# Norm squares stored in another token order, and an own timetable for the last group of a half

## The reference

```python
y = jnp.moveaxis(ys, 0, 1) + x * D[None, None, :, None]
yg = y.reshape(B, L, G, GROUP_SIZE)
var = jnp.mean(yg * yg, axis=-1, keepdims=True)
yn = (yg * lax.rsqrt(var + EPS)).reshape(B, L, I) * norm_weight
yn = yn * jax.nn.silu(gate)
out = jnp.einsum('bli,di->bld', yn, out_proj_w)
```

## Time and profile before

| | |
|---|---|
| time of 3 runs, median (lowest to highest) | 3199.41 us (3190.49 to 3212.25) |
| the profiled execution's own time | 3210.87 us |
| its span, first to last instruction | 3209.4 us |
| its mean granted TensorE clock | 0.975 |
| busy share PE / DVE / ACT / POOL | 95% / 67% / 52% / 20% |
| first half, second half, output block | about 0 to 1240, 1240 to 2473, 2473 to 3209 us |

### The profile page before, as it was taken

One profiled execution on the slowest core, in us unless ns is written; L12 is line 12 of the kernel. 1 busy time (PEld: TensorE's weight loads), 2 busy tenths in 40 slices (PEclk: granted clock), 3 DMA queues, 4 the chain that ended last, 5 costly groups with the idle time before them and its releaser, 6 DMA issues. The chain is left out here.

```text
span 3209.4 us, 44961 instructions
## 1 busy us (share of the span) xinstructions
PE 3064.5 (95%) x14304; PEld 2387.6 (74%) x14304; DVE 2155.3 (67%) x2660; ACT 1684.9 (52%) x3716; POOL 633.8 (20%) x447
## 2 busy tenths in 40 slices
PE   7999999999999994999999999999995999999998
PEld 6777777777777764777777777777773788888776
DVE  7666667675756664767666666767573887668877
ACT  3566574755656571475655756575563323234433
POOL 3222212121212223412112221212123000001112
PEclk9999999999999996999999999999997999999999
DMA  3434343343434333433352434334342444456565
GB/s 129 142 135 154 102 151 102 137 144 111 148 107 145 119 114 114 144 133 126 111 171 99 154 104 148 105 138 147 105 153 91 137 143 141 147 177 226 203 212 173
DMA packets 125815, 444.90 MB, mean 139 GB/s; under 512 B 17776, under 2 KB 22000, under 8 KB 109296
## 3 DMA queue, kind: packets, MB, share of 16 engines
q1 hardware_dynamic: 117840, 423.18, 39.4%
q0 software_dynamic: 4096, 14.68, 1.2%
q10 hardware_dynamic: 3744, 5.51, 0.5%
HBM read 397.90 MB, written 45.42 MB: 138 GB/s over the span
## 5 line engine op out<-in xcount | busy, mean ns | idle before, releaser
L935 PE MATMUL bank<-x_hi,w_hi 128*128 128x512 f32 x2560 | 1030.2, 402 | 7.3 <-DVE acc L692 7.3
L937 PE MATMUL bank<-x_hi,w_lo 128*128 128x512 f32 x2560 | 1005.5, 393 | 0.0
L936 PE MATMUL bank<-x_lo,w_hi 128*128 128x512 f32 x2560 | 1002.7, 392 | 0.0
L692 DVE SCALAR_TENSOR_TENSOR acc<-bank,conv_w,acc 128x511 f32<-128x511 f32 (+2 forms) x576 | 431.0, 748 | 352.9 <-ACT acc L521 325.5
L935 PEld LDWEIGHTS bank<-x_hi,w_hi 128*128 128x128 f32 x2560 | 484.3, 189 | 126.4 <-issue 21.8
L937 PEld LDWEIGHTS bank<-x_hi,w_lo 128*128 128x128 f32 x2560 | 484.3, 189 | 105.6
L936 PEld LDWEIGHTS bank<-x_lo,w_hi 128*128 128x128 f32 x2560 | 485.4, 190 | 95.3
L521 ACT ACTIVATE acc<-bank,tap_par 128x512 f32<-128x512 f32 x192 | 149.2, 777 | 654.7 <-PE bank L937 500.6
L1441 PE MATMUL bank<-wo_hi,y_hi 128*128 128x512 f32 x1024 | 401.4, 392 | 40.2 <-DVE wo_lo L1308 36.9
L1442 PE MATMUL bank<-wo_lo,y_hi 128*128 128x512 f32 x1024 | 400.0, 391 | 0.0
L1443 PE MATMUL bank<-wo_hi,y_lo 128*128 128x512 f32 x1024 | 399.8, 390 | 0.0
(11 more groups left out here) (153 smaller groups left out, 3394.8 us busy)
## 6 DMA issues: line engine op xcount, KB each, us to landing
attn<-cum_scratch SPq DMA_DIRECT2D x128, 1280.0 KB, 6.7
w_raw<-in_w_in SPq DMA_DIRECT2D x160, 512.0 KB, 3.6
y_raw<-y_scratch SPq DMA_DIRECT2D x128, 512.0 KB, 3.7
y_scratch<-gate SPq DMA_DIRECT2D x32, 1024.0 KB, 6.4
wo_raw<-in_w_out SPq DMA_DIRECT2D x128, 256.0 KB, 3.8
xbc<-in_x SPq DMA_DIRECT2D x16, 512.0 KB, 4.3
attn<-in_x SPq DMA_DIRECT2D x16, 512.0 KB, 3.7
rstd_b<-rc_scratch SPq DMA_DIRECT2D x32, 256.0 KB, 3.9
```

Of the source, the lines that this page charges most:

```text
L692: dve.scalar_tensor_tensor(acc[:, s % 2, back:], bank_proj[s % 2][:, 0:SEQ - back], mix.conv_w[:, g, m, 3 - back:4 - back], acc[:, s % 2, ...
L935: pe.matmul(out, w_hi[m % 2][:, k, :], hi, start=(k == 0), stop=False)
L936: pe.matmul(out, w_hi[m % 2][:, k, :], lo, start=False, stop=False)
L937: mm = pe.matmul(out, w_lo[m % 2][:, k, :], hi, start=False, stop=(k == KT - 1))
```

## The change

There are two parts. First, ScalarE writes each tile of squares in another order: token `4i + k` goes to column `128k + i`. It still reads `y` in token order, so 4 neighbouring results go 512 bytes apart each. GpSimd's sums are made column by column and are the same work. The weights of channel sum k are then the 128 neighbouring columns from `128k`.

Second, group 7 of each half gets its own plan `LAST`, with other slots for products, loads and exponentials. Products 3 to 7 stand one or two slots earlier (14, 16, 18, 20, 21 for 15, 17, 19, 21, 23), with what is derived from them. The exponentials have a list of their own, in which slots 11 and 18 hold two each.

```diff
-    def __init__(self, cb, load, mult, gate_from):
+    def __init__(self, cb, load, mult, gate_from, exp=None):
...
-        self.exp = [s - 3 + h for s in mult for h in range(2)]
+        self.exp = exp or [s - 3 + h for s in mult for h in range(2)]
...
-DRAIN = max(LATER.store) + 1
+LAST = Plan(cb=[4, 6], load=[4, 5, 7, 10, 12, 14, 15, 17], mult=[9, 11, 13, 14, 16, 18, 20, 21],
+            gate_from=CONV_SLOTS, exp=[6, 7, 8, 9, 10, 11, 11, 12, 13, 14, 15, 16, 17, 18, 18, 19])
+DRAIN = max(LAST.store) + 1
...
-            step(GROUPS - 1, LATER, LATER, True)
+            step(GROUPS - 1, LAST, LATER, True)
...
-                piece(GROUPS - 1, LATER, s)
+                piece(GROUPS - 1, LAST, s)
...
-                act.activation(out, y[:, u % 2, :], ACT.Square, scale=GC ** -0.5).then_inc(squared, 1)
+                act.activation(out.rearrange("p (k i) -> p i k", k=CHUNKS),
+                               y[:, u % 2, :].rearrange("p (i k) -> p i k", k=CHUNKS),
+                               ACT.Square, scale=GC ** -0.5).then_inc(squared, 1)
...
-                by_phase = sums[:, q, :].rearrange("p (i k) -> p k i", k=CHUNKS)
                 for k in range(CHUNKS):
-                    mm = pe.matmul(bank_y[q][:, k:k + 1], by_phase[:, k, :], one, start=True, stop=True)
+                    mm = pe.matmul(bank_y[q][:, k:k + 1], sums[:, q, k * P:(k + 1) * P], one, start=True, stop=True)
```

## The result

Over four runs of each kernel on one chip the time went from a median of 3196.74 us (3190.49 to 3212.25) to 3163.84 us (3159.40 to 3165.46). The ratio is 0.9891, with a 95% interval from 0.9866 to 0.9916: 1.1% faster. A second set on another chip gave 3162.26 us against 3198.03, ratio 0.9890 (0.9871 to 0.9908). The profiled execution took 3164.7 us, with a span of 3163.2. The forecast was 3163 us, between 3150 and 3182. The total came out right within 1 us, and that is in part luck: the timetable was worth less than its term, the channel sums a little more, and 2.8 us are explained by no term.

A forecast was written before the change was run, and what follows sets the result against it. TensorE, busy 95% of the span, was taken as the bound inside the groups. From the profiled execution, 3210.9 - 22.4 - 14.4 - 10.2 + 0.4 = 3164.3 us, stated as 3163 us, range 3150 to 3182.

The forecast's parts named there:

- The channel sums: On TensorE, neighbouring weight columns shorten loads, saving 0.8 us on each of 28 sums inside groups: 22.4 us (17 to 31).
- The falls: Drops of TensorE's clock to 0.5 behind channel sums following a product: all nine go, 1.6 us each, 14.4 us.
- The last group: At each half's end, unit 7's product starts 5.3 us sooner, less 0.2 for SP's queue: 10.2 us over two halves.
- the cover for its packed slots: Ahead of the drain, two exponential steps fit slots averaging 7.1 us: nothing charged; without that cover 3 us per half.
- `LAST` stalls an engine: Rival: ScalarE's packed slots delay gate work, or swapped DMAs cost most of 3.9 us; 3 us per half lost, 3169; 10%.
- The SP queue: In the drain, sequence 0's read back now stands behind sequence 1's store: 0.2 us a half charged, at worst 3.9.
- The strided write: ScalarE's scattered square write costs 0.2 us more each; two of 128 lie on a path: 0.4 us (0 to 0.8).

The follow-up runs named there:

- the doubled sums: The changed kernel with each channel sum computed twice from the neighbouring weights, same result: 3190.52 us over eight runs, 3191.33 in a one-run repeat.
- the exponentials moved: The changed kernel with one number changed in `LAST`, the first exponential step of unit 3 back from slot 11 to slot 12: 3158.06 us, ratio 0.9880.
- the timetable alone: The changed kernel with squares and weights put back as before, keeping only `LAST`: 3192.4 us against 3198.34 for the kernel before, ratio 0.9980.
- the strided read: The changed kernel with ScalarE's square reading `y` at a 16-byte stride and writing neighbouring columns: 3160.91 us against 3162.26.

## Why the prediction held, point by point

**The channel sums were right, slightly undersized.** Forecast: a pair 0.107 us apart in place of 0.207, 28 x 0.8 = 22.4 us. Measured: 0.101 behind a projection (0.81/8), so 16 x (1.66 - 0.81) + 12 x (1.89 - 0.92) = 25.2 us. The load's length came out as read from its unstrided neighbour, 192 against 190 ns. That this goes one for one into the time is shown by the doubled sums, and neighbouring groups stand 139.9 us apart where 140.1 was forecast. The Trainium skill (Advanced Engine Details and Errata, SBUF Cachelines) speaks of a penalty when each access goes to a different 16-byte line, and this pair of kernels agrees with it on the loads, 330 against 192 ns.

**The falls were right for the profiled execution and wrong for the median.** All nine went, worth 14.4 us there. That falls stay away behind the short sums is shown (none at 72 boundaries, against 21 at 48 with the strided ones); whether for their length or for their stride is open. The prediction guessed that the number of falls makes the runs' spread, and nonetheless took all nine off. Against a median run only some 5 to 6 us could be won. This didn't spoil the time forecast, as the sum was made against the slow execution that had the nine; it would have misled someone who put the same 14.4 us against the median. Between the execution with 9 falls and the first profile after, the output projection starts 2481.28 - 2435.57 = 45.7 us sooner, and the sum of terms was 46.6.

**The last group: the mechanism and its size were right, the cover for its packed slots wasn't.** Per half the forecast was 5.3 us less 0.2; the drain gives 5.2, and the last product takes 4.53 us behind a wait of 4.35, as assumed. The step that failed is "Ahead of the drain `LAST` packs ScalarE ... I charge nothing". It argued by the length of the slot, 7.1 us, and what bound was the order within it: the weight split stands behind the second step of exponentials (3.0 us), with VectorE's weighing behind that, which costs the product 1.2 us of wait; and this step at times waits for a table that hasn't landed, up to 1.5 us more. The rival *`LAST` stalls an engine* thus came true in part, by the double step that it named and a DMA wait that it didn't. It was priced at 3 us a half. Read at the start of the output projection, the timetable brings 2440.30 - 2430.32 = 10.0 us with the exponentials moved, as forecast (10.2), and 4.7 to 7.4 us as the change has it. The stall gives back 2.6 to 5.3 us over both halves, most of it in the first. The whole times agree: the timetable alone took 3187.23 us in its profile without a fall, 5.4 us less than the 3192.6 of the kernel before less its falls.

**The SP queue cost nothing**, where 0.2 us a half was charged. From the product of unit 7 to the read back (L338) it is 1195.92 - 1184.51 = 11.4 us against 1218.33 - 1207.37 = 11.0 before. Between the first store (L333, now L335) and this read back it is 1.41 us in both (1218.33 - 1216.92 and 1195.92 - 1194.51), so the 0.4 us more lies ahead of the queue, about what the longer square takes (0.45).

**The strided write was mis-sized, outside its own bounds.** Forecast 0.2 us a square, 0.4 at most; measured 0.50 (622 to 1121 ns), 0.98 ns per value. The bound came from a VectorE sum at 0.78 ns per value, and this is another engine. It cost little, because the step that decides was right: only two squares lie on a path, 0.9 us in all. Here the Trainium skill's rule on lines agreed in direction on both sides of ScalarE, as the strided read shows (1102 ns) beside the scattered write (1121 ns), and gives no size.

**What cancelled.** Against the sum of 3164.3 us for the profiled execution: the channel sums 2.8 us better, the last group 5.5 us worse (4.7 in place of 10.2), the squares 0.5 worse. That would be 3167.5; the profiled execution took 3164.7, and the 2.8 us between them aren't explained. Of these 0.8 (235.28 - 234.46) were won ahead of the first channel sum, which the change doesn't touch. Less their falls, executions of the kernel before differ by 3.9 us too (3196.5 and 3192.6 above). By the terms as measured the forecast would have been 4.5 us too low, well inside its range; so the match to 1 us is luck and the range is not. For the medians the same accounting is 25.2 for the sums, 5 to 6 for the falls, 4.7 to 7.4 for the last group and 0.9 back for the squares: 34 to 38 us, where 33 and 36 were measured.

## What to carry to other kernels

Read the weight loads apart from the matmuls: with one moving column the load was the cost here, and weights that lie in every fourth column doubled the time of a channel sum (0.207 us a pair against 0.101); move the stride to an engine that has room: ScalarE paid 60.7 us more in all, and 0.9 of it is found on a path. When a timetable is packed, look for what stands behind each moved step on its engine, and then for whether its input has landed, not for how full the slot is: one number in a list gave back 2.6 to 5.3 of the 10.0 us that the timetable was worth. And before something in one profile is counted as a gain, ask how often it happens: the falls of the clock were 9, 8 and 4 in three executions of one kernel.

## What the runs showed of the hardware

- ScalarE takes nearly as much longer over a 16-byte-stride read (1102 ns) as over a scattered write (1121 ns), against 622 ns for 512 neighbouring values.
- The falls of TensorE's granted clock to 0.5 differ in number between executions of one kernel, at the same instructions: 9, 8 and 4, each worth about 1.6 us. Most stand in consecutive groups; the profile with 4 also has two single ones.
- A stretch of one-column matmuls of 3.5 to 4.1 us was followed by a fall 26 times of 28, with neighbouring weights; one of 0.92 us never (72 boundaries).
- The wait of the last group's product doesn't sort the falls: the clock fell after 1.89, 2.23, 2.51 and 2.70 us, and not after nine waits of 1.20 to 1.65 us, nor after 2.21, 2.41 and 2.55.
